# Query-key and value products of attention in three fp32r terms instead of fp32

## What is computed

```python
q = jnp.einsum('btd,ed->bte', x, W_q)
k = jnp.einsum('btd,ed->bte', x, W_k)
v = jnp.einsum('btd,ed->bte', x, W_v)
scores = jnp.einsum('bqd,bkd->bqk', q, k) * scale
scores = jnp.where(causal, scores, -jnp.inf)
att = jax.nn.softmax(scores, axis=-1)
y = jnp.einsum('bqk,bkd->bqd', att, v)
out = jnp.einsum('btd,ed->bte', y, W_o)
```

## Time and profile before

| | us |
|---|---|
| median of 3 runs (lowest to highest) | 658.87 (658.45 to 660.17) |
| profiled execution | 659.68 |
| its span, first to last instruction | 657.8 |
| PE busy | 607.8 (92%) |
| DVE busy | 486.7 (74%) |
| ACT busy | 416.1 (63%) |
| POOL busy | 386.9 (59%) |

### The profile page before, as it was taken

One profiled execution on the slowest core, in us unless ns is written; L12 is line 12 of the kernel. 1 busy time (PEld: TensorE's weight loads), 2 busy tenths in 40 slices (PEclk: granted clock), 3 DMA queues, 4 the chain that ended last, 5 costly groups with the idle time before them and its releaser, 6 DMA issues. The chain is left out here.

```text
span 657.8 us, 15198 instructions
## 1 busy us (share of the span) xinstructions
PE 607.8 (92%) x4726; PEld 580.6 (88%) x4726; DVE 486.7 (74%) x1164; ACT 416.1 (63%) x732; POOL 386.9 (59%) x282
## 2 busy tenths in 40 slices
PE   1798999999988959999999999999999999999993
PEld 1697888888778959989999999999999999999983
DVE  7757668789788957667887778778788687867671
ACT  2814576766679747787756657566565665656660
POOL 5101111676675873556676676666767667688883
PEclk9999999999999979999999999999999999999998
DMA  8900010234588982853222131231312313121211
GB/s 344 306 31 1 22 44 33 83 115 153 194 295 290 264 221 51 272 168 60 35 51 46 32 64 33 49 48 32 64 34 44 54 32 62 28 43 25 34 25 16
DMA packets 37596, 62.47 MB, mean 95 GB/s; under 512 B 3696, under 2 KB 32944, under 8 KB 36400
## 3 DMA queue, kind: packets, MB, share of 16 engines
q1 hardware_dynamic: 16448, 36.19, 16.5%
q0 software_dynamic: 13296, 18.00, 15.1%
q10 hardware_dynamic: 7808, 7.74, 4.5%
HBM read 37.02 MB, written 24.89 MB: 94 GB/s over the span
## 5 line engine op out<-in xcount | busy, mean ns | idle before, releaser
L713 POOL TENSOR_TENSOR pj_lo<-w_ffn,pj_hi 128x1024 fp32r<-128x1024 f32 x66 | 163.2, 2476 | 88.1 <-ACT pj_hi L777 87.5
L1684 DVE TENSOR_TENSOR fc_lo<-w_ffn,fc_hi 128x1024 fp32r<-128x1024 f32 x78 | 113.6, 1489 | 55.7 <-ACT fc_hi L777 52.5
L702 POOL DMA_INDIRECT out<-y,add_id x71 | 111.4, 1569 | 46.3 <-issue 39.8
L777 ACT ACTIVATE pj_hi<-w_ffn 128x1024 fp32r x78 | 82.7, 1060 | 82.5 <-PE psO L2108 64.5
L2108 PE MATMUL psP<-pj_hi,h_hi 128*128 128x256 f32 x312 | 93.2, 299 | 6.7 <-DVE h_lo L1684 6.5
L777 ACT ACTIVATE fc_hi<-w_ffn 128x1024 fp32r x78 | 79.0, 1052 | 18.6 <-issue 18.6
L2108 PE MATMUL psP<-pj_lo,h_hi 128*128 128x256 f32 x312 | 88.3, 283 | 0.0
L2108 PE MATMUL psP<-pj_hi,h_lo 128*128 128x256 f32 x312 | 88.0, 282 | 0.0
L664 POOL DMA_INDIRECT slots<-rows,slot x64 | 67.8, 1059 | 21.8 <-issue 17.0
L2108 PE MATMUL psO<-pj_hi,h_hi 128*128 128x256 f32 x256 | 72.7, 284 | 0.0
L2108 PE MATMUL psO<-pj_lo,h_hi 128*128 128x256 f32 x256 | 72.5, 283 | 0.0
(11 more groups left out here) (365 smaller groups left out, 1610.4 us busy)
## 6 DMA issues: line engine op xcount, KB each, us to landing
w_ffn<-in_w_ffn SPq DMA_DIRECT2D x8, 2048.0 KB, 9.5
xg<-slots ACTq DMA_DIRECT2D x25, 265.0 KB, 2.9
xc<-in_x_ch SPq DMA_DIRECT2D x4, 1024.0 KB, 8.6
out<-x SPq DMA_DIRECT2D x16, 256.0 KB, 2.2
x<-in_x_tok SPq DMA_DIRECT2D x1, 3072.0 KB, 24.7
slots<-fill SPq DMA_DIRECT2D x9, 265.0 KB, 10.7
xg<-slots SPq DMA_DIRECT2D x7, 265.0 KB, 5.4
out<-y,add_id POOLq DMA_INDIRECT x71
```

The source lines that it names most:

```text
L702: nc.gpsimd.indirect_dma_start(out_d, bass.IndirectOffsetOnAxis(ap=add_id[:, s:s + 1], axis=0), y[:, s, :], None, compute_op=ALU.add).then ...
L713: nc.gpsimd.tensor_tensor(pj_lo[:, 4 * a:4 * a + 4, :], w_ffn[:, bass.ds(e, 1), (2 + a) * DFF:(3 + a) * DFF].rearrange("p a (c d) -> p (a ...
L777: nc.scalar.activation(out, src, ACT.Copy, **kw).then_inc(done, 1)
L1684: v.tensor_tensor(out, whole, upper.bitcast(F32), ALU.subtract).then_inc(done, 1)
```

## The change

Query-key and value products are made of upper and lower parts in fp32r (upper times upper, upper times lower, lower times upper), four fp32 calls becoming twelve fp32r calls in each of the two functions. The parts lie in a new area of SBUF that is taken from the end of the convolution's.

- Weights, once: ACT writes the query-key matrix rounded to fp32r (`qk_hi`) where it wrote it in fp32, and DVE subtracts to get `qk_lo`. In slot -1 ACT copies `vo_w` to `vo_hi`, and DVE subtracts to get `vo_lo`.
- Rows, for each batch: behind the copy to `xn_t`, ACT makes `xn_hi` from it, and DVE makes `xn_lo` (`normed_lower`, 128x512), between `attn_out(k - 1)` and `highest(k)` in its slot. There is one buffer of each, so ACT and DVE wait for `v_mm` of the batch before.
- PE: `query_keys(k)` also waits for `xn_lower`; slot 0 waits for the weights' parts.

```diff
             def normed_in(b):
                 act.wait_ge(t1_mm, b + 1)
                 if b > 1:
                     act.wait_ge(s_mm, b - 1)
+                if later(b):
+                    act.wait_ge(v_mm, b)
                 copy(xn_t[b % 2][:, :, :], psG[:, :], xnt_ready)
+                act.wait_ge(xnt_ready, b + 1)
+                copy(xn_hi[:, :, :], xn_t[b % 2][:, :, :], xn_upper)
...
+                if k == -1:
+                    act.wait_ge(ride_ready, 1)
+                    act.wait_ge(route_w, 1)
+                    copy(vo_hi[:, :, :], vo_w[:, :, :], vo_upper)
...
-            for n, (w, bank) in enumerate(((vo_w, psT1), (qk_w, psG))):
+            for n, (w, bank) in enumerate(((vo_w, psT1), (qk_hi, psG))):
...
+            def normed_lower(b):
+                if later(b):
+                    alone(v_mm, b)
+                dve.wait_ge(xn_upper, b + 1)
+                lower(xn_lo[:, :, :], xn_t[b % 2][:, :, :], xn_hi[:, :, :], xn_lower)
...
+                if k == -1:
+                    dve.wait_ge(vo_upper, 1)
+                    lower(vo_lo[:, :, :], vo_w[:, :, :], vo_hi[:, :, :], vo_lower)
+                if on(k + 1):
+                    normed_lower(k + 1)
                 if on(k):
                     highest(k)
...
+            dve.wait_ge(qkvo_ready, 2)
+            lower(qk_lo[:, :, :], psG[:, :].rearrange("p (h d) -> p h d", h=DH), qk_hi[:, :, :], qk_lower)
             dve.wait_ge(ld_x[0], 16)
             run_attention(dve, dve_slot)
...
             def query_keys(b):
                 pe.wait_ge(xnt_ready, b + 1)
+                pe.wait_ge(xn_lower, b + 1)
                 for a in range(DH):
-                    for hh in range(DH):
-                        ins = mm(psG[:, a * SEQ:(a + 1) * SEQ], qk_w[:, hh, a * P:(a + 1) * P], xn_t[b % 2][:, hh, :],
-                                 start=(hh == 0), stop=(hh == DH - 1))
+                    for n, (w, m) in enumerate(three(qk_hi, qk_lo, xn_hi, xn_lo)):
+                        for hh in range(DH):
+                            ins = mm(psG[:, a * SEQ:(a + 1) * SEQ], w[:, hh, a * P:(a + 1) * P], m[:, hh, :],
+                                     start=(n == 0 and hh == 0), stop=(n == 2 and hh == DH - 1))
...
                 for s, bank in enumerate((psV, psT2)):
-                    for hh in range(DH):
-                        ins = mm(bank[:, 0:VW], xn_t[b % 2][:, hh, s * P:(s + 1) * P], vo_w[:, hh, :],
-                                 start=(hh == 0), stop=(hh == DH - 1))
+                    for n, (w, m) in enumerate(three(xn_hi, xn_lo, vo_hi, vo_lo)):
+                        for hh in range(DH):
+                            ins = mm(bank[:, 0:VW], w[:, hh, s * P:(s + 1) * P], m[:, hh, :],
+                                     start=(n == 0 and hh == 0), stop=(n == 2 and hh == DH - 1))
...
                 if k == 0:
-                    pe.wait_ge(qkvo_ready, 2)
+                    pe.wait_ge(qk_lower, 1)
+                    pe.wait_ge(vo_upper, 1)
+                    pe.wait_ge(vo_lower, 1)
```

More of the change, by code:

```diff
@@ L149, in hybrid_block @@
         SENT_BYTES = 36064
+        PARTS_BYTES = 4 * DH * D * 4 + 2 * DH * VW * 4
         end = (nc.sbuf_usable_end - start - 64) // 32 * 32
@@ L162, in hybrid_block @@
             "sent": (weights_at + LATE * EXPERT - SENT_BYTES, weights_at + LATE * EXPERT),
-            "conv": (weights_at + LATE * EXPERT, end),
+            "conv": (weights_at + LATE * EXPERT, end - PARTS_BYTES),
+            "parts": (end - PARTS_BYTES, end),
         }
@@ L244, in hybrid_block @@
         idft_parts = at("idft_parts", [3 * MC, D], F32R)
-        qk_w = at("qk_w", [P, DH, D])
+        qk_hi, qk_lo = (place("parts", n, [P, DH, D], F32R) for n in ("qk_hi", "qk_lo"))
+        vo_hi, vo_lo = (place("parts", n, [P, DH, VW], F32R) for n in ("vo_hi", "vo_lo"))
+        xn_hi, xn_lo = (place("parts", n, [P, DH, SEQ], F32R) for n in ("xn_hi", "xn_lo"))
         vo_w = at("vo_w", [P, DH, VW])
@@ L349, in hybrid_block @@
             sem(n) for n in ("stats_ready", "mv_ready", "var_ready", "roots_ready", "shift_ready"))
+        qk_lower, vo_upper, vo_lower, xn_upper, xn_lower = (
+            sem(n) for n in ("qk_lower", "vo_upper", "vo_lower", "xn_upper", "xn_lower"))
         t1_mm, xnt_ready, g_mm, gt_ready, v_mm, v_ready, s_mm = (
@@ L1039, in _, with lower @@
             v = nc.vector
+            def lower(out, whole, upper, done):
+                v.tensor_tensor(out, whole, upper.bitcast(F32), ALU.subtract).then_inc(done, 1)
             def alone(s, value):
@@ L1681, in expert_of @@
                 return dve.value_load(table[0:1, 0, bass.ds(g, 1)], min_val=0, max_val=E - 1)
-            def lower(out, whole, upper, done):
-                v.tensor_tensor(out, whole, upper.bitcast(F32), ALU.subtract).then_inc(done, 1)
             def fc_lower(g, par, e, parts=range(DH)):
@@ L1924, in transposes @@
                     pe.wait_ge(gt_ready, b)
+                else:
+                    pe.wait_ge(qk_lower, 1)
                 for hh in range(DH):
```

## The result

The changed kernel takes 667.17 us (median of 4 runs, 666.04 to 667.51), the kernel before beside it 659.52: a ratio of 1.0119, 95% interval 1.0100 to 1.0138. That is 7.8 us on 658 (the two medians differ by 7.65). The profiled execution took 666.93 us, its span is 664.8.

What follows compares the result with a forecast made beforehand. PE was taken to set the pace, with DVE close behind in routing slots (2.0 us to spare). Start 3.9, light slots 0, routing slots 0.75 and 2.5, slot 14 -0.5 gave +6.6 us: 665.5 us, range 660.5 to 670.

Steps and rivals of the forecast that it cites:

- PE's saving: Query-key and value products on PE: 3.06 us instead of 3.56, saving 0.50 us a slot, bounds 0 to 0.6.
- Light slots: Slots 1 to 4, 8 and 13: 7.60 us as before, PE's saving becoming a 0.50 us wait ahead of `query_keys`.
- The start: Slots -1 and 0: lower parts behind `spec_of` put `query_keys(0)` at 61.6 and `query_keys(1)` at 69.5, +3.9 us in all.
- rival 3: PE's clock falls in the new wait ahead of `query_keys(0)`: another 3.3 us, or 669 us; chance 0.15.
- Slots 5 to 7 and 9 to 12: Routing slots, DVE's queue setting the pace: +0.75 us (lowest +0.4) and +2.5 us (lowest +1.5).
- rival 2: The experts' wait for their rows at 241 us swallows the later attention: no change, about 659.5 us; chance 0.09.
- Rival 1: DVE's subtraction stays off the path and PE still bounds the slots: -3.1 us, or 655.8 us; chance 0.05.
- rival 5: Three terms save PE no time; light slots, first slot and slot 14 lose 0.5 us each: 669.5 us; chance 0.04.
- Rival 4: The subtraction waits for POOL's `roots`, 0.7 us more in each of a dozen slots: 674 us; chance 0.07.

Runs made afterwards that it cites:

- experiment 1: Changed kernel with DVE's subtraction of the rows made for the first batch only, PE reusing that part: 658.58 us, ratio 1.0013 to the kernel before.
- experiment 5: Changed kernel with DVE's subtraction ahead of `attn_out` from slot 0 on, not behind it: 663.50 us, ratio 1.0077 to the kernel before.
- Experiment 3: Changed kernel plus 10 matmuls ahead of PE's wait in slot 0 and 5 in slot 1: 662.72 us, ratio 1.0074 to the kernel before.
- experiment 2: Changed kernel with all splits, copies and waits kept but the two products in fp32 as before: 674.98 us, ratio 1.0254 to the kernel before.
- experiment 4: Changed kernel with both lower parts ahead of `spec_of(1, 1)` and `(1, 2)`, and `spec_of(1, 3)` ahead of `conv_out(2)`: 661.87 us, ratio 1.0071.
- experiment 6: Changed kernel with the edits of experiment 4 and experiment 5 together: 658.34 us, ratio 1.0018 to the kernel before.
- experiment 7: Kernel of experiment 6 with POOL instead of DVE making the rows' lower part in slots 0 to 7: 660.09 us, ratio 1.0038.
- Experiments 8 to 10: Second expert's weights ordered before the early scatter wait, in the kernel before, the changed one and that of experiment 6: 661.28, 669.66, 660.46 us.

## Why the prediction was right, point by point

The forecast was +6.6 us, and attention ended 8.2 us later, the span 7.0. The mechanism held: a subtraction that DVE can't hide takes PE's saving and more. Single terms were off, in both directions.

- **PE's saving.** 0.55 us in a light slot, 0.50 forecast. It can be taken at 0.63 where PE doesn't stop (experiment 1). My upper bound of 0.6 was short, because behind other fp32 work the first pair also starts 0.18 us sooner.
- **Light slots.** 7.58 us for the forecast 7.60, with waits of 0.36 to 0.44 us (0.78 in slot 8's). Experiments 1 and 5 show the cause from both sides: without the subtraction, or with it ahead of `attn_out`, the same slots take 6.9 to 7.0.
- **The start.** Its first step was exact (61.67, forecast 61.6). `query_keys(1)` was forecast at 69.5 and came at 70.92. Experiment 3 shows that step to be right but for the clock: 69.68 with the clock at 1.00.
- **The clock** (rival 3, chance 0.15) came true on top of the forecast: two falls in slots 0 and 1 cost 2.7 us together, where I had priced one at 3.3. I had set it beside the forecast as another outcome, and it is a term that adds to it. My reading of the earlier trace rows, 4.9 us into a wait, was also too kind, since it fell a second time after a wait of 2.49 us, and a third time after 2.42 us, at the start of the experts.
- **Slots 5 to 7 and 9 to 12.** +0.42 and +1.68 instead of +0.75 and +2.5, both near the lower bounds that I gave. "DVE doesn't wait, and its queue sets the slot" held as to the flagged waits, of which slots 5 to 7 have none left. Its terms were too large. A subtraction costs 0.60 us there, from its start to that of `highest` (109.49 to 110.09), not 0.65. And the gap ahead of `conv_out`, too short to be flagged, shrank: from `highest` to `conv_out` slots 5 and 6 take 4.06 and 4.01 us instead of 4.13. In slots 9 to 12 POOL's wait of 0.5 us vanished as well. Nor is DVE the only pace: in slot 6 `conv_out` starts 0.53 us behind `idft_of`, as in a light slot, and experiment 2 shows the products on the path at 0.4 us a slot as soon as they take longer.
- **The experts** (rival 2). Not the whole shift, as the rival had it, but 1.1 us was given back, 0.3 of it up to the wait for `xg`. The wait itself shrank by 3.1 us; longer waits for `h_lo` and the clock's third fall took most of that again. In experiment 5 1.8 us of the 4.9 were given back. What sets this wait isn't settled. In the two kernels and experiments 1 and 3 to 7 the rows land 22.7 to 23.4 us behind the order of the fifth expert's weights. That order comes three loads behind the first group's gather, and the gather waits for POOL's scatters. Why each of the three steps takes 10.5 to 15.4 us stays open. Experiments 8 to 10 showed only that bringing the second load forward delays the gather, and that PE then waits for it.
- **Rival 1** fell with the light slots, **rival 5** with experiment 2.
- **Rival 4** fell in this kernel: the subtraction took its 0.68 us in slots where `roots` run, as in slot 6, where `roots` ran from 116.45 to 117.77 and the subtraction from 117.07 to 117.75. The Trainium skill, "SBUF — State Buffer", section "Who interferes with whom", calls the port that the two engines share an exclusive lock, and says that the order of issue decides who blocks. For a subtraction that comes second the trace disagrees: it took 0.68 us in all 13 slots in which it started while `roots` ran. In the other order it agrees in kind: in experiment 5 `roots` start 0.17 us into the subtraction and take 1.69 us instead of 1.32. And experiment 7 agrees with what the same section of the Trainium skill says of `tensor_scalar`, that it can contend with GpSimd: `variances` waited out POOL's instruction. So the contention exists; the change's order of work just didn't meet it.

The errors of the clock (+2.6 against the forecast), the heavy slots (-1.2) and the experts (-1.1) partly cancel. So the mechanism was right, but that the total came this near was in part luck.

## What to carry to other kernels

Where one engine prepares the operands of another, price the preparation by its place in the queue first: the same 0.68 us cost all of PE's saving behind `attn_out`, and none of it in the light slots ahead of it. Elsewhere moving the work can move the cost instead of saving it (slots 12 to 14 in experiment 5). Put the time at half clock behind a new wait of PE into the sum as a term with a chance of its own, and not as another outcome: here it cost 1.3 to 1.7 us in a slot, behind every wait of 4.5 us that a trace shows and behind some of those of 1.8 to 2.7 us. An engine that never waits in a stretch isn't yet its only pace: look for what ends the gaps that no view flags.

## What the runs showed that was not expected

The granted clock fell with PE at work. In experiment 4 PE stopped at about 57.2, resumed at 59.39, and the clock went from 1.00 to 0.50 (2.4 to 1.2 GHz) near 60.8, 1.4 us after it had resumed; in slot 1 of the changed kernel it fell near 71.5, 0.5 us after PE had resumed from its wait of 2.49 us. The same wait didn't always end in the same way. Ahead of slot 13 the clock stayed at 1.00 behind 1.86 us in the changed kernel and fell behind 1.84 us in experiment 4; ahead of slot 1 it stayed at 1.00 behind 2.54 us in experiment 5. Waits of 0.96 us and less left it at 1.00. What decides between the two isn't shown, and with executions that differ in it, a difference of 1.5 us between two profiles can be the clock alone.

DVE and POOL held each other up in some pairs and not in others, and who came second didn't tell which: `variances` (128x4) took 1.17 us instead of 0.17 inside POOL's 128x512 subtraction, `roots` 1.69 instead of 1.32 behind a DVE subtraction, and a DVE subtraction of two inputs in SBUF inside `roots` its usual 0.68. Slot 6 of the changed kernel:

```profile
116.45 1.32 POOL L660 TENSOR_TENSOR roots<-ve,power 128x6 f32<-128x6 f32 x1 [6.26 <-DVE ve L1228]
...
117.07 0.68 DVE L1056 TENSOR_TENSOR xn_lo<-xn_t,xn_hi 128x512 fp32r<-128x512 f32 x1
```
